# The router's logits computed in the attention's program instead of in a block of their own

## The chip, the core and the metric

One NeuronCore of one Trainium2 chip runs the whole kernel. The time is device microseconds of one execution; for each kernel the median of several runs counts. Five engines work side by side, each through its own list of instructions: TensorE (PE; its weight loads are shown as PEld), VectorE (DVE), ScalarE (ACT), GpSimd (POOL) and SyncE (SP), which here only issues DMAs. They wait for each other through semaphores.

## What is computed

A decoder layer on 64 sequences of 128 tokens, width 256, that is 8192 rows: causal self-attention with 16 heads, residual and layer norm; cross-attention, residual and layer norm; then a mixture of 8 experts (two per token, limited capacity), residual and layer norm.

```python
x = _layernorm(x + attn(x, w_in, w_out))
x = _layernorm(x + xattn(x, ctx, ctx, Wq, bq, Wk, bk, Wv, bv, Wo, bo))
# inside the expert part:
probs = softmax(x @ Wr + br, axis=-1)      # Wr is 256 x 8: the logits
gates, ids = top_k(probs, 2)
```

The change is about `x @ Wr + br`, which stands between the second layer norm and the choice of experts.

## The kernel before, in words

`decoder_layer` runs three stages one after the other: `attention_layers` (both attentions), `logits_block`, and `moe` (`route_block` and the experts). Each is a `Block`: a program for every engine, with a barrier at its end, so that no engine begins the next block before all have finished this one.

**Attention.** The rows are worked on in groups of 512 (G). There are 16 groups a layer, so 32 in all (`groups`), 64 half-groups (`halves_of`, indexed by u) and 128 sets of heads and rows (`sets`, indexed by k). The order of the instructions is written out by hand in each engine's program. Behind the loop over the sets stand the last steps. On TensorE (lines 470 to 475): `weigh(127)`, `set_back(126)`, `output(62)`, `set_back(127)`, `output_back(63)`, `output(63)`. A half-group ends so: TensorE turns the normalised heads back (`output_back`), ScalarE copies them as fp32r (`copy_out`), VectorE makes the rest (`rest_o`), TensorE multiplies with the output weights (`output`), VectorE adds the residual and takes the statistics (`residual`, `deviation`), GpSimd makes the inverse deviation, and ScalarE scales (`normalise`). SyncE stores the half-group to two tensors in HBM, `rows` and `total` (`store`, line 157).

SyncE's queue is in order. In the last group (g = 31) it calls `load_for_logits` (line 189): the identity, the router's matrix, the bias, and the first four groups of finished rows (`LOGIT_LOADS` = 4, 512 KB each). Then it issues the stores of half-groups 62 and 63 and waits for the landing of the last four stores, and the block ends.

**Logits.** `logits_block` (line 853) has 16 groups of 512 rows. A group takes these steps: TensorE turns the rows with 8 transposes into two PSUM banks (line 925, `lg_T`); ScalarE copies both as fp32r (line 950); VectorE subtracts for the rests (line 969); TensorE multiplies with the matrix, split into two parts, in 4 matmuls (`logits_of`, line 904); ScalarE adds the bias (line 943); TensorE turns the result back (`back`, line 914); VectorE adds the two parts (`take`, line 959). TensorE's order is turn(g), logits_of(g-1), back(g-2). The matrix is split on VectorE at the start of the block (lines 961 to 965), and TensorE waits for that before its first transpose. SyncE loads groups 4 to 15 into a ring of four, each when the group four before it has been turned (line 884), and then clears 128 spare rows of both tensors and loads `iota8` (lines 887 to 889).

PSUM has eight banks. The attention uses all of them (`A` has four, `B` and `C` two each), and so does the logits' block.

Of the kernel before, what the change touches and what calls it, by code (L numbers as in the profile page):

```python
# [38 lines left out]
def attention_layers(nc, layer_groups, x_in, x_turned, ctx_turned, x1, x2_outs, w_self, w_cross, consts, logits_inputs):  # L39
# [7 lines left out]
    with ExitStack() as c:  # L47
# [48 lines left out]
        C = [c.enter_context(nc.psum_tensor(f"{tag}C{i}", [P, G], FP32)) for i in range(2)]  # L96

# [41 lines left out]
        def _(sp):  # L139
# [59 lines left out]
            for g in range(groups):  # L199
# [19 lines left out]
        def _(pe):  # L219
# [598 lines left out]
E = 8  # L818
# [34 lines left out]
def logits_block(nc, tiles, rows_dram, sum_dram, inputs, logits, iota8, iota8_dram):  # L853


    groups = tiles // NB
    LOADS = LOGIT_LOADS
    with ExitStack() as c:
        wr_s = c.enter_context(nc.sbuf_tensor("lg_wr_s", [P, HALVES, 2, E], FP32R))
        zero = c.enter_context(nc.sbuf_tensor("lg_zero", [P, D + E], FP32))  # L860
        xT = c.enter_context(nc.sbuf_tensor("lg_xT", [P, 2, 2, HALVES, G], FP32R))
        lT = c.enter_context(nc.sbuf_tensor("lg_lT", [2 * E, 2, G], FP32))
        tb = [c.enter_context(nc.psum_tensor(f"lg_T{i}", [P, G], FP32)) for i in range(4)]
        lb = [c.enter_context(nc.psum_tensor(f"lg_L{i}", [2 * E, G], FP32)) for i in range(2)]
        bb = [c.enter_context(nc.psum_tensor(f"lg_B{i}", [P, NB, 2, E], FP32)) for i in range(2)]
        ident, wr, br, x2, const_in, x_loaded = (inputs[name] for name in ("ident", "wr", "br", "x2", "const_in", "x_loaded"))
        wr_hi = c.enter_context(nc.semaphore("lg_wr_hi"))
        wr_ready = c.enter_context(nc.semaphore("lg_wr_ready"))
        zero_made = c.enter_context(nc.semaphore("lg_zero_made"))
        zeroed = c.enter_context(nc.semaphore("lg_zeroed"))  # L870
        t_full = c.enter_context(nc.semaphore("lg_t_full"))
        a_copied = c.enter_context(nc.semaphore("lg_a_copied"))
        d_copied = c.enter_context(nc.semaphore("lg_d_copied"))
        l_full = c.enter_context(nc.semaphore("lg_l_full"))
        l_done = c.enter_context(nc.semaphore("lg_l_done"))
        b_full = c.enter_context(nc.semaphore("lg_b_full"))
        b_done = c.enter_context(nc.semaphore("lg_b_done"))
        block = c.enter_context(nc.Block())

        @block.sync  # L880
        def _(sp):
            for g in range(LOADS, groups):
                sp.wait_ge(t_full, g - LOADS + 1)
# [6 lines left out]
            sp.wait_ge(zeroed, 48)  # L890

        @block.tensor
        def _(pe):
            pe.wait_ge(const_in, 48)
            pe.wait_ge(wr_ready, 1)

# [1137 lines left out]
```

## Time and profile before

| | us |
|---|---|
| median of 3 runs | 1586.39 |
| lowest, highest | 1585.27, 1587.44 |
| profiled execution | 1587.09 |
| its span, first to last instruction | 1585.4 |
| mean granted TensorE clock, share of full | 0.946 |

Busy over the span: TensorE 90%, VectorE 64%, ScalarE 63%, GpSimd 39%.

| stretch of the trace, us | stage |
|---|---|
| 0 to 921 | attention, both layers |
| 921 to 924 | last stores land, barrier |
| 924 to 965 | logits |
| 965 to 1071 | routing |
| 1071 to 1585 | experts |

A row of the timeline gives the start and the length of an instruction, or of several of one kind in a row (x8), its engine, its line in the kernel, the tile written and the tiles read. In brackets stands how long the engine had been idle before it, and what ended that. PEclk is TensorE's granted clock as a share of 2.4 GHz.

### The profile page before, as it was taken

To read this page: it belongs to the slowest core of one execution; us is meant where nothing else is said; L and a number is where in the kernel's file an instruction comes from. 1 tells how busy PE (TensorE), PEld (TensorE's weight loads), DVE (VectorE), ACT (ScalarE), POOL (GpSimd) and SP (SyncE) were. 2 spreads that over 40 slices of the span, in tenths; PEclk is the share of its full clock that TensorE was granted. 3 is DMA by queue.
4 is the path that set the end of the run, shared out by engine and by line. 5 is a ranking of instruction groups with operands and counts; after the bars stand their busy time and mean duration, and the time that the engine had idled before them with its cause. 6 is when DMAs were issued, how large, how long until landed. Compare 5 with 4: busy or idle time off the path is not lost. (4 is left out here: it accounts for less than half of the span.)

```text
span 1585.4 us, 43757 instructions
## 1 busy us (share of the span) xinstructions
PE 1424.7 (90%) x17886; PEld 1198.1 (76%) x17886; DVE 1019.1 (64%) x2266; ACT 990.9 (63%) x1456; POOL 619.9 (39%) x688
## 2 busy tenths in 40 slices
PE   7999999999999999999999773158999999999990
PEld 5777777777777777777777652048999999999980
DVE  5666666666677777777777647884454454454582
ACT  4677777777777677777767554205565565565563
POOL 2644444454452322222232100013455455455485
PEclk9999999999999999999999976558999999999995
DMA  6021222122221222222221174003443443443464
GB/s 195 22 62 62 62 62 61 44 61 62 62 62 57 82 66 82 82 82 82 74 79 43 58 212 102 0 11 101 97 105 48 99 102 49 100 103 50 97 240 180
DMA packets 115142, 130.72 MB, mean 82 GB/s; under 512 B 26650, under 2 KB 97084, under 8 KB 114944
## 3 DMA queue, kind: packets, MB, share of 16 engines
q1 hardware_dynamic: 100288, 106.18, 21.5%
q0 software_dynamic: 14656, 21.74, 7.9%
q8 instruction: 144, 2.36, 0.6%
q14 instruction: 54, 0.44, 0.1%
HBM read 83.73 MB, written 44.16 MB: 81 GB/s over the span
## 5 line engine op out<-in xcount | busy, mean ns | idle before, releaser
L527 ACT ACTIVATE at_pr<-at_A 128x2048 f32<-128x2048 f32 x128 | 240.8, 1881 | 145.5 <-PE at_A L347 145.5
L622 DVE TENSOR_REDUCE at_mx<-at_A 128x12 f32<-128x1536 f32 x128 | 224.7, 1755 | 57.6 <-PE at_A L312 54.0
L767 POOL TENSOR_SCALAR_AFFINE_SELECT at_pr<-at_pr 128x2048 f32<-128x2048 f32 x64 | 128.6, 2010 | 204.9 <-ACT at_pr L527 204.8
L1839 POOL DMA_INDIRECT total<-ex_o,ids x70 | 115.8, 1654 | 187.5 <-DVE ex_o L1767 172.5
L1708 DVE TENSOR_TENSOR ex_hT<-ex_h,ex_hT 128x384 fp32r<-128x384 f32 (+1 forms) x192 | 113.0, 589 | 98.9 <-ACT ex_hT L1641 84.9
L658 DVE TENSOR_TENSOR at_oT<-at_C,at_oT 128x512 fp32r<-128x512 f32 x64 | 44.3, 692 | 164.9 <-ACT at_oT L540 164.9
L347 PE MATMUL at_A<-at_qp,at_kt 32*128 32x256 f32 x2048 | 139.8, 388 | 0.0
L362 PE MATMUL at_C<-at_pr,at_v 128*32 128x128 f32 x4096 | 138.3, 276 | 1.0 <-ACT at_oq L534 1.0
L1640 ACT ACTIVATE ex_h<-ex_U,ex_b 128x384 f32<-128x384 f32 (+1 forms) x192 | 116.3, 606 | 33.3 <-PE ex_U L35 27.4
L362 PEld LDWEIGHTS at_C<-at_pr,at_v 128*32 128x32 f32 x4096 | 104.0, 109 | 43.3 <-issue 42.1
L35 PE MATMUL ex_U<-ex_xT,ex_w_even 128*128 128x384 f32 (+1 forms) x576 | 115.3, 360 | 5.1 <-ACT ex_hT L1641 3.5
L774 POOL TENSOR_SCALAR at_shift<-at_mv 128x2 f32<-128x2 f32 x64 | 14.7, 230 | 264.9 <-DVE at_mv L686 262.3
L35 PE MATMUL ex_D<-ex_w_even,ex_hT 128*128 128x256 f32 (+1 forms) x960 | 117.2, 281 | 0.2
L35 PE MATMUL ex_D<-ex_w_odd,ex_hT 128*128 128x256 f32 (+1 forms) x960 | 116.6, 281 | 0.3
L35 PEld LDWEIGHTS ex_D<-ex_w_even,ex_hT 128*128 128x128 f32 (+1 forms) x960 | 115.1, 184 | 1.8 <-DVE ex_raw L1762 1.5
L1615 ACT CAST ex_xT<-ex_T 128x384 fp32r<-128x384 f32 (+1 forms) x46 | 21.0, 507 | 152.5 <-PE ex_T L1559 150.6
L35 PEld LDWEIGHTS ex_D<-ex_w_odd,ex_hT 128*128 128x128 f32 (+1 forms) x960 | 115.1, 184 | 1.4 <-DVE ex_raw L1762 0.9
L1641 ACT ACTIVATE ex_hT<-ex_U,ex_b 128x384 fp32r<-128x384 f32 (+1 forms) x192 | 114.7, 597 | 0.0
L35 PEld LDWEIGHTS ex_U<-ex_xT,ex_w_even 128*128 128x128 f32 x576 | 106.6, 195 | 10.0 <-ACT ex_hT L1641 3.9
L35 PE MATMUL ex_U<-ex_xT,ex_w_odd 128*128 128x384 f32 (+1 forms) x576 | 111.0, 351 | 0.0
L35 PE MATMUL at_B<-at_wo,at_oT 128*128 128x256 f32 x768 | 108.0, 290 | 1.4 <-DVE at_oT L658 1.4
L1823 POOL DMA_INDIRECT ex_xg<-rows,ids x77 | 97.5, 1266 | 28.6 <-issue 21.5
(245 smaller groups left out, 3067.9 us busy)
## 6 DMA issues: line engine op xcount, KB each, us to landing
ex_w_in<-in_w SPq DMA_DIRECT2D x16, 1024.0 KB
at_turned<-in_x_turned SPq DMA_DIRECT2D x16, 512.0 KB, 4.6
at_x<-in_x SPq DMA_DIRECT2D x16, 512.0 KB, 4.0
x<-at_y SPq DMA_DIRECT2D x32, 256.0 KB, 2.3
at_x<-x SPq DMA_DIRECT2D x16, 512.0 KB, 3.9
at_turned<-in_ctx_turned SPq DMA_DIRECT2D x16, 512.0 KB, 4.6
rows<-at_y SPq DMA_DIRECT2D x32, 256.0 KB, 2.2
total<-at_y SPq DMA_DIRECT2D x32, 256.0 KB, 3.1
```

Source lines behind the costliest of these rows:

```text
L35: last = nc.tensor.matmul(out, pick_l(left, a), pick_r(right, b), start=(start and n == 0), stop=(stop and n == 2))
L347: last = nc.tensor.matmul(A[:, i, n, :, :], kt[rows, g % 2, half, tok], qp[rows, g % 2, half, :, tok], start=False, stop=(n == 1), skip_gr ...
L362: last = nc.tensor.matmul(b[32 * j:32 * j + VW, (2 * n + quad) * P:(2 * n + quad + 1) * P], v[:, g % 2, 2 * np_ + n, half * HEADS_HALF + 4 ...
L527: nc.scalar.activation(pr[:, k % 2].rearrange("p i n a q -> p (i n a q)"), A[:].rearrange("p i n a q -> p (i n a q)"), ACT.Exp).then_inc(e ...
L622: nc.vector.tensor_reduce(mx[:, k % 2, 0:12], A[:, 0:3].rearrange("p i n a k -> p (i n a) k"), AX, ALU.max).then_inc(max_done, 1)
L658: nc.vector.tensor_tensor(oT[:, u % 2, 1].rearrange("p t n -> p (t n)"), C[1][:, :], oT[:, u % 2, 0].rearrange("p t n -> p (t n)").bitcast ...
L767: nc.gpsimd.affine_select(out=t, in_=t, compare_op=ALU.is_ge, fill=0.0, base=0, pattern=[[0, 16], [1, P]], channel_multiplier=-1).then_inc ...
L1640: nc.scalar.activation(h[:, m % HR, 0:n], U[m % UP][:, 0:n], ACT.Silu, bias=b1[:, j, m:m + 1])
L1641: nc.scalar.activation(hT[:, par(j, ch), 0, m, 0:n], U[m % UP][:, 0:n], ACT.Silu, bias=b1[:, j, m:m + 1]).then_inc(u_done, 1)
L1708: nc.vector.tensor_tensor(hT[:, par(j, ch), 1, m, 0:n], h[:, m % HR, 0:n], hT[:, par(j, ch), 0, m, 0:n].bitcast(FP32), ALU.subtract).then_ ...
L1823: nc.gpsimd.indirect_dma_start(xg[0:n, xg_of(s), b, :], None, rows_dram, bass.IndirectOffsetOnAxis(ap=ids[0:n, e, at:at + 1], axis=0), bou ...
L1839: nc.gpsimd.indirect_dma_start(sum_dram, bass.IndirectOffsetOnAxis(ap=ids[0:n, e, at:at + 1], axis=0), o[0:n, pr, b, :], None, bounds_chec ...
```

## The change

- The logits' programs become functions (`logits_programs`) that `attention_layers` calls from its own engine programs. The block `logits_block` and its barrier are gone. The PSUM banks of the logits are those of the attention: the turned rows lie in `A`, the logits in `B[1]` and `C[0]`, their transposes in `C[1]` and `B[0]`. The turned copies `xT` use the attention's `sT`.
- Groups 0 and 1 are turned, copied and split between the attention's last steps. The other 14 groups follow behind these steps, in the same order as before.
- `load_for_logits` is called in the group before the last (`groups - 2`).
- The clearing of the spare rows and the load of `iota8` move up, to between the last two stores; so do the loads of groups 4 and 5. The other loads follow the last store.
- The matrix is split behind `normalise_set(126)`. Before its third turn TensorE waits for the last residual.

```diff
@@ SyncE, in attention_layers
-                if g == groups - 1:
+                if g == groups - 2:
                     load_for_logits()
+            def load_later(i):
+                for u in (2 * (layer_groups + i), 2 * (layer_groups + i) + 1):
+                    sp.wait_ge(y_stored[u % 4], stored_before(u + 4))
+                load_rows(sp, i)
+
             store(halves_of - 2)
+            clear_rest(sp)
+            load_later(LOGIT_LOADS)
+            load_later(LOGIT_LOADS + 1)
             store(halves_of - 1)
+            for i in range(LOGIT_LOADS + 2, layer_groups):
+                load_later(i)
             for u in range(halves_of - 4, halves_of):
                 sp.wait_ge(y_stored[u % 4], stored_before(u + 4))
+            rest_cleared(sp)
@@ TensorE
             set_back(sets - 1)
+            turn_rows(pe, 0)
             output_back(halves_of - 1)
+            turn_rows(pe, 1)
             output(halves_of - 1)
+            tensor_program(pe, lambda engine: engine.wait_ge(res_done, halves_of))
@@ ScalarE
             copy_o(sets - 1)
+            copy_rows(act, 0)
             copy_out(halves_of - 1)
             normalise(halves_of - 2)
-            normalise(halves_of - 1)
+            copy_rows(act, 1)
+            scalar_program(act, lambda: normalise(halves_of - 1))
@@ VectorE
             normalise_set(sets - 2)
+            split_matrix(dve)
             residual(halves_of - 2)
             deviation(halves_of - 2)
             normalise_set(sets - 1)
+            rest_of_rows(dve, 0)
             rest_o(halves_of - 1)
+            rest_of_rows(dve, 1)
             residual(halves_of - 1)
             deviation(halves_of - 1)
+            vector_program(dve)
@@ new, in logits_programs
+    def load_rows(sp, g):
+        sp.wait_ge(turned, g - LOADS + 1)
+        sp.dma_start(x2[:, g % LOADS], rows_dram[g * G:(g + 1) * G, 0:D] ...
+    def clear_rest(sp):
+        sp.wait_ge(wr_ready, 1)
+        sp.dma_start(rows_dram[groups * G:groups * G + P, :], zero[:]).then_inc(zeroed, 16)
+        sp.dma_start(sum_dram[groups * G:groups * G + P, :], zero[:, 0:D]).then_inc(zeroed, 16)
+        sp.dma_start(iota8[:], iota8_dram).then_inc(zeroed, 16)
+    def tensor_program(pe, last_sum):
...
+        pe.wait_ge(wr_ready, 1)
+        logits_of(0)
+        last_sum(pe)
+        for g in range(2, groups):
+            turn_rows(pe, g)
+            logits_of(g - 1)
+            back(g - 2)
+        logits_of(groups - 1)
+        back(groups - 2)
+        back(groups - 1)
+    def scalar_program(act, last_normalise):
...
+        add_bias(0)
+        last_normalise()
+        for g in range(2, groups):
+            copy_rows(act, g)
+            add_bias(g - 1)
+        add_bias(groups - 1)
+    def vector_program(dve):
...
+        for g in range(2, groups):
+            rest_of_rows(dve, g)
+            take(g - 2)
+        take(groups - 2)
+        take(groups - 1)
@@ decoder_layer
-            logits_block(nc, tokens // P, rows, total, inputs, logits, iota8, ins["iota8"])
```

`turn_rows`, `copy_rows`, `rest_of_rows`, `logits_of`, `back`, `add_bias` and `take` hold the instructions of the old block for one group, with the waits they had.

## Rows read from the trace of the kernel before

**Rows 1.** Busy time of each engine by stretch, with granted clock (PEclk) and DMA

```profile
core 0: us, PE busy (x) PEld busy (x) DVE busy (x) ACT busy (x) POOL busy (x), PEclk, DMA share, GB/s
...
909.09:911.11 2.02, 0.00 (x1) 0.01 (x1) 1.86 (x7) 0.00 (x0) 0.45 (x2) 1.00 0.44 70
911.11:913.16 2.05, 0.65 (x4) 0.41 (x4) 0.69 (x1) 1.36 (x3) 0.91 (x2) 0.69 0.97 336
913.16:916.09 2.93, 2.93 (x12) 2.64 (x12) 0.00 (x0) 0.21 (x1) 0.00 (x0) 0.50 1.07 308
916.09:924.15 8.06, 0.01 (x1) 0.00 (x0) 1.70 (x6) 1.09 (x2) 1.36 (x4) 0.50 0.55 189
924.76:928.85 4.09, 3.65 (x17) 3.28 (x18) 1.29 (x2) 1.48 (x3) 0.00 (x0) 0.50 0.21 43
928.85:932.87 4.02, 4.02 (x29) 2.75 (x29) 2.68 (x5) 2.98 (x6) 0.00 (x0) 0.99 0.91 249
932.87:965.23 32.36, 30.89 (x215) 19.94 (x213) 18.95 (x42) 21.93 (x40) 0.00 (x0) 1.00 0.60 168
```

**Rows 2.** Timeline (start, us, engine line op) of TensorE over the attention's last steps

```profile
906.97 1.68 PE L35 MATMUL at_B<-at_wo,at_oT 128*128 128x256 f32 x12
...
911.11 0.66 PE L387 MATMUL at_C<-at_ident,at_on 128*128 128x128 f32 x4 [2.02 <-DVE at_on L653]
...
913.16 2.93 PE L35 MATMUL at_B<-at_wo,at_oT 128*128 128x256 f32 x12 [1.40 <-DVE at_oT L658]
```

**Rows 3.** Timeline of VectorE and ScalarE over the same steps

```profile
908.69 0.69 DVE L671 TENSOR_TENSOR at_y<-at_B,at_x 128x512 f32<-128x512 f32 x1 [0.72 <-PE at_B L35]
...
911.80 0.59 ACT L540 CAST at_oT<-at_C 128x512 fp32r<-128x512 f32 x1 [4.58 <-PE at_C L387]
...
912.28 1.09 ACT L545 ACTIVATE at_y<-at_y,at_shift,at_rstd 128x256 f32<-128x256 f32 x2
912.42 0.69 DVE L658 TENSOR_TENSOR at_oT<-at_C,at_oT 128x512 fp32r<-128x512 f32 x1 [1.36 <-ACT at_oT L540]
...
916.13 0.69 DVE L671 TENSOR_TENSOR at_y<-at_B,at_x 128x512 f32<-128x512 f32 x1 [3.02 <-PE at_B L35]
...
919.60 1.09 ACT L545 ACTIVATE at_y<-at_y,at_shift,at_rstd 128x256 f32<-128x256 f32 x2 [6.23 <-POOL at_shift L779]
```

**Rows 4.** Timeline of the logits block, from its first copy

```profile
926.79 1.07 ACT L950 CAST lg_xT<-lg_T 128x512 fp32r<-128x512 f32 x2 [6.10 <-PE lg_T L925]
927.41 1.29 DVE L969 TENSOR_TENSOR lg_xT<-lg_T,lg_xT 128x512 fp32r<-128x512 f32 x2 [2.75 <-ACT lg_xT L950]
...
930.86 1.07 ACT L950 CAST lg_xT<-lg_T 128x512 fp32r<-128x512 f32 x2 [0.19 <-PE lg_T L925]
...
932.87 1.17 PE L904 MATMUL lg_L<-lg_xT,lg_wr_s 128*16 128x512 f32 x4
...
934.32 1.09 PE L925 MATMUL lg_T<-lg_ident,lg_x 128*128 128x128 f32 x8
...
960.39 1.17 PE L904 MATMUL lg_L<-lg_xT,lg_wr_s 128*16 128x512 f32 x4
```

**Rows 5.** Timeline of the SyncE queue around the moved issues

```profile
896.23 0.36 SPq L161 DMA_DIRECT2D rows<-at_y  x1
...
913.40 0.36 SPq L161 DMA_DIRECT2D rows<-at_y  x1
...
920.72 0.36 SPq L161 DMA_DIRECT2D rows<-at_y  x1
...
951.89 0.50 SPq L887 DMA_DIRECT2D rows<-lg_zero  x1
...
952.44 1.32 SPq L888 DMA_DIRECT2D total<-lg_zero  x1
```

**Rows 6.** DMAs of line L196, the first four loads of rows, issue to landing

```profile
DMA to landing us min/median/max: 3.6/5.5/7.4
```

**Rows 7.** DMAs of line L884, the twelve later loads of rows, issue to landing

```profile
DMA to landing us min/median/max: 3.5/3.9/4.9
```

More of the change, by code:

```diff
@@ new lines, in rest_cleared, with turn_rows @@
+    def rest_cleared(sp):
+        sp.wait_ge(zeroed, 48)
+    def turn_rows(pe, g):
+        if g == 0:
+            pe.wait_ge(const_in, 48)
+        pe.wait_ge(x_loaded[g % LOADS], 16 * (g // LOADS + 1))
+        if g >= 2:
+            pe.wait_ge(d_copied, 2 * (g - 1))
+        for half in range(HALVES):
+            for n in range(NB):
+                last = nc.tensor.matmul(T[2 * (g % 2) + half][:, n * P:(n + 1) * P],
+                                        x2[:, g % LOADS, n, half * P:(half + 1) * P], ident[:],
+                                        start=True, stop=True, is_transpose=True)
+        last.then_inc(turned, 1)
@@ new lines, in tensor_program, with logits_of, back @@
+    def tensor_program(pe, last_sum):
+        def logits_of(g):
+            pe.wait_ge(a_copied, 2 * g + 2)
+            pe.wait_ge(d_copied, 2 * g + 2)
+            if g >= 2:
+                pe.wait_ge(l_done, g - 1)
+            for part in range(2):
+                for t in range(HALVES):
+                    last = nc.tensor.matmul(lb[g % 2], wr_s[:, t, :, :].rearrange("p a e -> p (a e)"),
+                                            xT[:, g % 2, part, t, :],
+                                            start=(part == 0 and t == 0), stop=(part == 1 and t == HALVES - 1))
+            last.then_inc(l_full, 1)
+        def back(g):
+            pe.wait_ge(l_done, g + 1)
+            if g >= 2:
+                pe.wait_ge(b_done, g - 1)
+            for n in range(NB):
+                last = nc.tensor.matmul(bb[g % 2][:, n, :, :].rearrange("p a e -> p (a e)"), lT[:, g % 2, n * P:(n + 1) * P],
+                                        ident[0:2 * E, 0:2 * E],
+                                        start=True, stop=True, is_transpose=True)
+            last.then_inc(b_full, 1)
+        pe.wait_ge(wr_ready, 1)
[8 more added lines that the diff above has]
+        back(groups - 1)
@@ new lines, in copy_rows, with add_bias @@
+    def copy_rows(act, g):
+        if g == 0:
+            act.wait_ge(const_in, 48)
+        act.wait_ge(turned, g + 1)
+        if g >= 2:
+            act.wait_ge(l_full, g - 1)
+        for half in range(HALVES):
+            nc.scalar.copy(xT[:, g % 2, 0, half, :], T[2 * (g % 2) + half]).then_inc(a_copied, 1)
+    def scalar_program(act, last_normalise):
+        def add_bias(g):
+            act.wait_ge(l_full, g + 1)
+            if g >= 2:
+                act.wait_ge(b_full, g - 1)
+            nc.scalar.activation(lT[:, g % 2, :], lb[g % 2], ACT.Identity, bias=br[:, 0:1]).then_inc(l_done, 1)
+        add_bias(0)
[4 more added lines that the diff above has]
+        add_bias(groups - 1)
@@ new lines, in split_matrix, with rest_of_rows @@
+    def split_matrix(dve):
+        nc.vector.memset(zero[:], 0.0)
+        dve.wait_ge(const_in, 48)
+        nc.vector.tensor_copy(wr_s[:, :, 0, :], wr[:]).then_inc(wr_hi, 1)
+        dve.wait_ge(wr_hi, 1)
+        nc.vector.tensor_tensor(wr_s[:, :, 1, :], wr[:], wr_s[:, :, 0, :].bitcast(FP32), ALU.subtract).then_inc(wr_ready, 1)
+    def rest_of_rows(dve, g):
+        for half in range(HALVES):
+            dve.wait_ge(a_copied, 2 * g + half + 1)
+            nc.vector.tensor_tensor(xT[:, g % 2, 1, half, :], T[2 * (g % 2) + half],
+                                    xT[:, g % 2, 0, half, :].bitcast(FP32), ALU.subtract).then_inc(d_copied, 1)
@@ new lines, in vector_program, with take @@
+    def vector_program(dve):
+        def take(g):
+            dve.wait_ge(b_full, g + 1)
+            nc.vector.tensor_reduce(logits[:, g * NB:(g + 1) * NB, :], bb[g % 2].rearrange("p n a e -> p n e a"),
+                                    AX, ALU.add).then_inc(b_done, 1)
+        for g in range(2, groups):
[3 more added lines that the diff above has]
+        take(groups - 1)
+    return load_rows, clear_rest, rest_cleared, turn_rows, tensor_program, copy_rows, scalar_program, split_matrix, rest_of_rows, vector_program
```

136 lines of the change are left out of this document (24 added, 112 removed).

## The prediction

> **What bounds the kernel now.** I began with the busy time by stretch, because an average over the whole kernel hides the seam between attention and router [rows 1]. Up to 909 us TensorE is busy and its clock is at 1.00 (2.4 GHz). Then come 15 us in which it does little: 0.00 busy in 2.02, 0.65 in 2.05, one product of 2.93 us at a clock of 0.50 (1.2 GHz), and 0.01 busy in the 8.06 us to 924.15. Only after that does the logits' work start, again at 0.50, and from 932.87 it runs 32.36 us with TensorE busy for 30.89.
>
> The timelines then say what each part waits for. In the attention's tail a single half-group goes round: transpose back at 911.11, copy at 911.80, rest at 912.42, output product at 913.16, residual at 916.13, last normalise at 919.60 [rows 2, 3]. That is a chain of dependences, with every engine mostly idle. In the logits' loop the product of one group begins 2.29 us after that of the one before it ((960.39 - 932.87) / 12), and TensorE has no gap there, so TensorE sets the pace [rows 4]. The seam between them is pure delay: the last normalise ends at 920.69, and the copies of the third group of rows, the first point from which the loop runs evenly, start at 930.86 [rows 3, 4]. Those 10.2 us hold two stores and their landing, the barrier, the matrix split, and groups 0 and 1 turned at the half clock.
>
> **The change part by part.** All starts of the new kernel are estimates, worked out from the rows named, on the clock of the trace of before.
>
> *Loads one group sooner.* Three constants and four loads of 512 KB are issued after the store of half-group 59, near 884 us. The next store comes at 896.23 [rows 5] and the slowest of these loads took 7.4 us [rows 6], so they have landed before anything asks for them. Cost nothing; cover some 8 us. They also leave the queue free later.
>
> *Matrix split* (VectorE: a clear, a copy, a subtraction of small tiles). It goes in front of the residual at 908.69, before which VectorE sat 0.72 us idle [rows 3]. The first loop step of the old block cannot begin until this is done (TensorE started at 924.76, the block at 924.15 [rows 1]), so it took at most 0.6. It fits: cost nothing, 0.6 if the cover were gone.
>
> *Group 0 turned, copied, split.* Eight transposes at full clock take 1.09 [rows 4] and go from about 909.1 into the 2.02 us in which TensorE is idle [rows 1]: done by 910.2, before output_back at 911.11. ScalarE copies for 1.07, 910.2 to 911.3, before copy_out at 911.80: 0.5 us to spare. VectorE subtracts for 1.29 from about 911.1 (it has just released output_back) to 912.4, and rest_o starts at 912.42 [rows 3]. This is the thinnest cover, nearly zero; I book 0.0, with 0.3 as the upper bound if a copy is late.
>
> *Group 1.* Transposes follow output_back, 911.8 to 912.9; output starts at 913.16, so hidden. ScalarE's copies stand behind normalise(62), which runs 912.28 to 913.37, so they run 913.3 to 914.4. Rests follow 0.62 after the copies (927.41 against 926.79 [rows 4]) and take 1.29: 913.9 to 915.15. Here VectorE is late for once: the residual that it must do next is queued behind them.
>
> *The last output product.* At full clock it takes 1.68, as at 906.97; it took 2.93 at half clock [rows 2]. The clock fell after TensorE had been idle 2.02 us and busy 0.65 of the following 2.05 [rows 1]. The 16 transposes fill both gaps to about 0.9 us idle and 0.3 us idle, so I take the full clock. The product then ends at 914.84 rather than 916.09, the residual could start at 914.9, and starts at 915.1 behind the rests: 1.0 sooner than 916.13. All that follows up to the last normalise keeps its 3.47 us, so that starts at 918.6.
>
> *The seam.* ScalarE goes straight from normalise(63) to the copies of group 2. Two instructions in a row overlap by 0.1 (912.28 against 911.80 + 0.59 [rows 3]), so these start at 918.6 + 1.09 - 0.1 = 919.6 instead of 930.86: **11.3 us sooner**. Of this 10.3 is the seam and 1.0 the clock. Behind the output product TensorE has logits(0) 1.17, then the wait for the last residual (about 915.8), turn(2) 1.09, logits(1) 1.17, back(0) 0.4 and turn(3) 1.09 [rows 4]. It is through near 919.6, and logits(2) comes 2.01 after the copies as before (932.87 - 930.86), at 921.6. Thus ScalarE's last normalise sets the start of the loop; TensorE waits 2 us for it.
>
> *The loop.* From there its operations, order and depth are the same, the rest is 32.36 us in both, and the route and expert stages start from the same state. They shift as a block.
>
> *SyncE's queue.* The store of half-group 62 (913.40) is now followed by the three clearing DMAs and the loads of groups 4 and 5; the last store stands behind these. The clears took 0.50 and 1.32 for two of them [rows 5]; with some 0.5 for each other issue the queue is free near 917.8, and the last store's data are ready at 919.7. Cost nothing; cover 1.9 us. No engine waits for that store but the loads issued behind it.
>
> *Rows in time.* Load 4 is issued near 916.8 and needed at 934.32 - 11.3 = 923.0 [rows 4]. The landings are 3.5 to 4.9 in the loop [rows 7] and up to 7.4 with four in a row [rows 6]: 920.7 to 924.2. Load 6 must follow the last store, so it is issued near 920.7, and is needed two periods later than load 4, at 927.6; it lands between 924.2 and 928.1. I take the median of the rows where loads queue, 5.5, since the last store's 512 KB lie before it: no wait. Upper end 1.2 us.
>
> The Trainium skill ("DMA: Bandwidth & Descriptors", Queues, rings and completion order) says that each DMA engine consumes its descriptors in ring order, which speaks against this arrangement: load 6 cannot pass the last store. This trace does not show the order by itself. By the skill's fixed cost of about 2.0 us and 27 GiB/s for each of 16 engines an estimate for 1 MB is 4.3 us, which would put load 6 at 925.0, in time; the sum would not change.
>
> **Sum.** 1587.09 (the profiled execution: span 1585.4 and 1.7 around it) - 11.3 = 1575.8. The median of the three runs, 1586.39, is 0.7 below the profiled execution, so for the median: **1575.1 us**.
>
> **Rivals.**
>
> *The clock falls in the new gap.* My own sum leaves TensorE idle for 2 us between turn(3) and logits(2), as long as the gap of 2.02 after which it fell before. Against it: here 6 us of dense work stand before and TensorE stays busy after. Where it falls, TensorE sets the pace and pays: the 16 first transposes took 3.65 at half clock [rows 1] against 2 x 1.09. It rose again after 4 us of work (from 924.76 to near 928.9, 0.99 in the next stretch). Loss: 4.1 x (1 - 2.18 / 3.65) = 1.7. Time 1576.8.
>
> *The clock falls where it did.* If the transposes do not hold it, the output product stays 2.93 and the residual starts at 916.13: the gain is the seam alone, 10.3. The rests of group 1 are then covered. TensorE has 16 transposes and two products behind it at half clock, but 3 us of waiting to absorb them. Time 1576.1. For it: what I add is small work. Against: it was at 1.00 up to 909 with gaps.
>
> *A late load.* Load 4 or 6 holds the loop for up to 1.2: 1576.3.
>
> *Slower than before.* TensorE runs the whole loop at 0.50, for instance after a fall at the new gap from which it does not rise. A period would be 2.29 x 3.65 / 2.18 = 3.8, 1.5 more for each of 14 groups, 21 in all, less 11.3: 1596. It decides from the point where 8 groups run at half clock (8 x 1.5 = 12). Against it: in the trace it rose after 4 us of such work, and stayed up.
>
> *The change does nothing for time.* This would need the last store's landing or the barrier to lie on the path still. ScalarE has no wait between normalise(63) and the copies but for the turned rows, so only a hidden stall at the end, where SyncE waits for clears issued 35 us earlier, could do so. I see none. Time 1586.4.
>
> **How the numbers follow.** Forecast 0.50; fall in the gap 0.24; fall as before 0.12; late load 0.06; slower 0.02; nothing gained 0.02; and 0.04 for a later stage that moves by a few us for reasons not in these rows. A measurement of this kernel tells about 0.2% (3.2 us) from no change. Faster by more takes all the first four and half of the last: 0.94; same 0.03; slower 0.03. The range takes in both clock cases, the late load on top of either, and the 1.1 us by which single runs of before lie around their median: 1573.4 to 1578.2.
>
> **What would show it.** In the new profile: PEclk 1.00 over the output product and its length 1.68; the last residual near 915.1 and the last normalise near 918.6; copies of group 2 within 1.0 us of that start; logits(2) near 921.6; a period of 2.29; the block's end near 953.9; the expert stage as long as before. The prediction is wrong if VectorE's rests push rest_o beyond 912.7, if a turn waits for its rows, or if the period is longer.

## The result, and the profile after

| | before | after |
|---|---|---|
| median of 6 runs each, us | 1586.32 | 1578.65 |
| lowest, highest | 1585.27, 1587.77 | 1574.62, 1581.2 |
| ratio, with its 95% interval | | 0.9949 (0.9934 to 0.9965) |
| profiled execution | 1587.09 | 1579.99 |
| its span | 1585.4 | 1578.2 |
| mean granted clock of TensorE | 0.946 | 0.948 |

The change gives 7.7 us, where 11.2 were forecast, and 1578.65 lies 0.45 above the top of the range. The six runs also lie further apart (6.6 us) than those of before (2.5 us), and their times go with their clocks: the fastest, 1574.62, ran at a mean of 0.951, the slowest, 1581.2, at 0.947.

The last steps of the attention in the changed kernel, as a timeline (start, length, engine and line, tiles, count; in brackets the idle time and what ended it). It answers to [rows 2, 3].

```profile
908.98 1.04 PE L918 MATMUL at_A<-lg_ident,lg_x 128*128 128x128 f32 x8
...
911.03 1.28 DVE L989 TENSOR_TENSOR at_sT<-at_A,at_sT 128x512 fp32r<-128x512 f32 x2
...
911.66 1.04 PE L918 MATMUL at_A<-lg_ident,lg_x 128*128 128x128 f32 x8
...
912.48 0.69 DVE L677 TENSOR_TENSOR at_oT<-at_C,at_oT 128x512 fp32r<-128x512 f32 x1 [0.17 <-ACT at_oT L557]
...
913.23 1.70 PE L35 MATMUL at_B<-at_wo,at_oT 128*128 128x256 f32 x12 [0.53 <-DVE at_oT L677]
...
915.14 0.68 DVE L690 TENSOR_TENSOR at_y<-at_B,at_x 128x512 f32<-128x512 f32 x1
...
918.60 1.09 ACT L562 ACTIVATE at_y<-at_y,at_shift,at_rstd 128x256 f32<-128x256 f32 x2 [2.03 <-POOL at_shift L802]
919.60 1.05 ACT L964 CAST at_sT<-at_A 128x512 fp32r<-128x512 f32 x2
...
921.58 1.87 PE L931 MATMUL at_B<-at_sT,lg_wr_s 128*16 128x512 f32 x4 [2.31 <-ACT at_sT L964]
```

Both turns sit in the gaps, the output product takes 1.70 instead of 2.93, the last normalise starts at 918.60, the copies of group 2 at 919.60 and the product of group 2 at 921.58. The forecast said 918.6, 919.6 and 921.6. Yet that product takes 1.87, not 1.09 or 1.17.

The same stretches as [rows 1], of the changed kernel:

```profile
core 0: us, PE busy (x) PEld busy (x) DVE busy (x) ACT busy (x) POOL busy (x), PEclk, DMA share, GB/s
909.20:911.15 1.95, 0.82 (x8) 0.58 (x6) 1.85 (x8) 1.04 (x2) 0.45 (x2) 1.00 0.05 13
911.15:913.20 2.05, 1.53 (x12) 1.29 (x12) 1.85 (x3) 1.38 (x4) 0.91 (x2) 1.00 0.01 3
913.22:915.00 1.78, 1.77 (x14) 1.62 (x15) 1.06 (x2) 1.18 (x3) 0.00 (x0) 1.00 0.38 133
919.25:921.55 2.30, 0.02 (x1) 0.00 (x0) 1.36 (x3) 2.30 (x5) 0.00 (x0) 0.94 1.02 358
921.55:928.05 6.50, 6.47 (x24) 3.56 (x24) 2.87 (x6) 2.79 (x6) 0.00 (x0) 0.50 0.73 211
928.05:956.80 28.75, 27.29 (x189) 17.78 (x188) 16.30 (x36) 18.94 (x35) 0.00 (x0) 1.00 0.50 142
```

The clock holds through the attention's tail. It falls in the gap of 2.3 us between turn(3) and logits(2): TensorE then starts only 24 matmuls in the next 6.50 us, at 0.50. This is the first rival of the prediction, with a longer stretch at half clock than it allowed.

To compare executions part by part I measure from fixed marks in each timeline: **A**, from ScalarE's first normalise of the last group of rows (half-group 60) to that of half-group 61; **B**, from the same start to the router's first instruction on ScalarE (the part the change is about, A included); **E**, the experts' start, from the first product into `ex_U` to the first into `ex_D`.

| trace | start of A | A | B | E | span |
|---|---|---|---|---|---|
| before | 895.11 | 10.52 | 70.41 | 26.16 | 1585.4 |
| after | 893.67 | 12.02 | 63.42 | 27.06 | 1578.2 |

From B's end to the experts' first product it is 105.61 and 105.66, and from the first product into `ex_D` to the end 488.11 and 488.39. So the 7.2 us of span are: B 6.99 less, everything ahead of the last group 1.44 less, E 0.90 more, and 0.33 more in the rest.

B should have lost 11.3. A holds 1.5 of what is missing: A is work that the change doesn't touch, and in it the clock fell. First before, then after:

```profile
895.11:905.63 10.52, 8.27 (x163) 6.46 (x166) 5.88 (x15) 6.16 (x8) 1.36 (x4) 1.00 0.15 52
```

```profile
893.67:905.69 12.02, 9.76 (x163) 7.85 (x166) 5.89 (x15) 6.16 (x8) 1.36 (x4) 0.86 0.13 46
```

and its product at the start, on the timeline:

```profile
894.18 2.91 PE L35 MATMUL at_B<-at_wo,at_oT 128*128 128x256 f32 x12
```

The work is the same on every engine and only TensorE's part is longer, with an output product of 2.91. The 1.44 us ahead of the last group are a fall too, one that the trace of before has near its start and the other has not (0.76 against 1.00). It comes and goes with the execution: of the 19 traces of this study the 10 that have it reach the last group at 894.12 to 895.12, and those without it at 893.36 to 893.86, or at 894.23 in one with another fall just ahead. First before, then after:

```profile
8.00:15.00 7.00, 4.38 (x12) 3.45 (x13) 6.51 (x14) 1.27 (x2) 1.42 (x1) 0.76 1.05 377
```

```profile
8.00:15.00 7.00, 4.58 (x19) 3.23 (x18) 6.57 (x14) 1.86 (x3) 1.48 (x1) 1.00 1.06 383
```

E has two slow groups of 24 products in both kernels. The first opens it (6.54 before, 6.86 after), while the clock is still at the 0.50 of the routing. The second stands at its end, behind a wait of 3.53 and 3.00; it takes 6.04 before and 6.97 in the changed kernel, where a group at full clock takes 4.46. First before, then after:

```profile
1071.13 6.54 PE L35 MATMUL ex_U<-ex_xT,ex_w_even 128*128 128x384 f32 x24 [1.58 <-PEq L992]
...
1091.41 6.04 PE L35 MATMUL ex_U<-ex_xT,ex_w_even 128*128 128x384 f32 x24 [3.53 <-ACT ex_hT L1641]
```

```profile
1062.75 6.86 PE L35 MATMUL ex_U<-ex_xT,ex_w_even 128*128 128x384 f32 x24 [1.58 <-PEq L1021]
...
1083.00 6.97 PE L35 MATMUL ex_U<-ex_xT,ex_w_even 128*128 128x384 f32 x24 [3.00 <-ACT ex_hT L1670]
```

### The profile page after: what moved, and what is told of

Its sections match the earlier page's. It is cut to its first block and busy times, and to the rows that moved or that the text cites. A ratio compares the mean times of both kernels' runs of the same rounds, so it can differ in the third digit from the quotient of the medians.

```text
span 1578.2 us, 43757 instructions
## 1 busy us (share of the span) xinstructions
PE 1427.3 (90%) x17886; PEld 1198.4 (76%) x17886; DVE 1019.1 (65%) x2266; ACT 991.2 (63%) x1456; POOL 619.4 (39%) x688
```

## The experiments

**My theory:** the seam is worth the 11.3 us of the forecast, and what is missing is TensorE's clock: a fall in the new gap, and in this execution one in the last group. **Rivals:** the loop or the loads cost more than booked; the interleaved steps hold up the attention's tail; the experts' start is worse with this kernel. A, B and E are taken from one profiled execution of each kernel; medians and ratios from its timed runs. All kernels below compute the whole result. Where products of zeros are added, they write into a PSUM bank that nobody reads just then.

### The same kernel again, and with the new gap filled

The first kernel is the changed one, unaltered. The second fills the gap with ten products of zeros (`FILL` = 10), 512 columns each, behind turn(3):

```diff
             turn_rows(pe, g)
+            if g == 3:
+                for _ in range(FILL):
+                    nc.tensor.matmul(L[0][:, :], warm[:, 0:P], warm[:, :], start=True, stop=True)
             logits_of(g - 1)
```

> The changed kernel again, beside the others, for more of its times with their clocks. The gap theory (TensorE idles 2.3 us before the product of group 2, and in some executions its clock falls to 0.50 there for one or two stretches of 3.4 us) expects a median of 1576 to 1580, a spread of 5 us or more, and times that go with the mean granted clock: in the six runs so far 0.951 gave 1574.6 and 0.947 gave 1580.6 to 1581.2. A rival that puts the spread on the transfers expects times that do not go with the clock.

> Ten products of zeros (512 columns each, 2.1 us at full clock) stand in the 2.3 us gap behind the fourth turn; nothing else changes. Gap theory: PEclk is 1.00 from 909 to the end of the logits, the last product of the logits comes 37 us after the last normalise begins or sooner (it was 955.27 + 0.42 - 918.60 in the changed kernel with the fall, 2.6 less without), and the median is 1 to 2.5 us below the changed kernel's. Rival, that the fall has its cause before the gap or is only a matter of when the chip looks: it falls as before, and the products of zeros at half clock cost up to 2 us more. Rival, that the loop lost its time to late rows: no change from the changed kernel.

Measured: the changed kernel 1570.46 against 1581.87 of the kernel before beside it, ratio 0.9940 (0.9926 to 0.9953), 11.4 us. Filled: 1570.22, 0.9928 (0.9914 to 0.9941), 11.65 us. The medians do not tell them apart, though 1 to 2.5 us were expected; the spread does, 4.8 us against 1.4. The median of the unaltered kernel was expected at 1576 to 1580. But the kernel before takes 4.5 us less here too than in the first comparison, so I take this for another chip (which one the first comparison ran on is not on record; all later ones are).

The trace of this execution of the changed kernel is the case without a fall. The product behind the gap takes 1.09, and in the 6.54 us from there TensorE starts 45 matmuls where it started 24 in 6.50:

```profile
919.77 1.09 PE L931 MATMUL at_B<-at_sT,lg_wr_s 128*16 128x512 f32 x4 [2.31 <-ACT at_sT L964]
```

```profile
917.45:919.76 2.31, 0.01 (x1) 0.02 (x1) 1.38 (x3) 2.31 (x5) 0.00 (x0) 1.00 1.03 358
919.76:926.30 6.54, 6.53 (x45) 4.23 (x46) 4.07 (x9) 4.53 (x9) 0.00 (x0) 1.00 0.96 277
```

With the gap filled:

```profile
917.12 1.09 PE L918 MATMUL at_A<-lg_ident,lg_x 128*128 128x128 f32 x8
918.05 2.32 PE L955 MATMUL at_B<-at_warm 128*128 128x512 bf16 x10
920.53 1.08 PE L933 MATMUL at_B<-at_sT,lg_wr_s 128*16 128x512 f32 x4 [0.16 <-issue]
```

| trace | A | B | E |
|---|---|---|---|
| changed kernel, no fall | 10.52 | 59.10 | 20.78 |
| gap filled | 10.52 | 59.10 | 20.88 |

70.41 - 59.10 = **11.31 us**: with the clock up, the change brings what the sum said. The fill costs nothing: the product after it waits 0.16, and starts 26.41 behind the start of A in both traces.

### More executions of the changed kernel

One trace with a fall and one without say little on how often it comes, so the pair was run again on three more chips (9, 2 and 11; the runs above are from chip 1), the last time with the waits of the last group filled too (the edit is shown further down).

> The changed kernel once more, beside the kernel with its gap filled and the one with the copies first, for a comparison within one call (the first call found 11.4 us and the blind runs 7.7 us of gain). Gap theory: 7 to 11.5 us below the kernel before, with a spread of 4 us or more; executions with the higher mean clock are the faster ones. From the last group's first normalise to the first instruction of the routing the trace shows 59.1 us if the clock stays up, 60.6 if it falls in the last group, about 62 if it falls in the gap, 63.4 if in both (before: 70.4).

> The changed kernel with ten products of zeros in the gap. Gap theory: its slowest executions are faster than the slowest of the changed kernel by 2 us or more, its fastest equal to the fastest of the changed kernel within 0.5 us, its median 0 to 3 us lower. Rival, that the difference of 3.6 us between the first two comparisons came from the chips alone: same median and same spread as the changed kernel.

> The changed kernel a third time. 7.5 to 11.5 us below the kernel before. If the smaller gain of the blind runs belonged to chips on which the experts' start stalls (26 us from the first to the last of their first-layer products instead of 21), a chip of that kind gives 7 to 9 and one of the other kind 9.5 to 11.5; if it was the chance of where the clock falls, either kind gives either.

> The gap filled. Gap theory: 1 to 3 us below the changed kernel on a chip with that stall, and no execution slower than the changed kernel's slowest less 2 us. From the last group's first normalise to the routing 59.1 us, or 60.6 if the clock falls in the last group.

> The changed kernel a fourth time. On a chip with the stall at the experts' start (kernel before near 1586): 7 to 10 us of gain and times spread over 4 us or more, if the two places in which the clock falls are the reason for the blind runs' 7.7. On one without it: 9.5 to 11.5, as three times before.

> The changed kernel with both places filled (ten products of zeros in the gap, 19 in the last group's waits), beside the changed kernel on the same chip. 11 to 11.7 us below the kernel before on either kind of chip, spread 2 us or less. If the kind of chip, not the clock, made the blind runs' shortfall: no better than the changed kernel beside it.

| run | before beside it | this | ratio (95%) | A | B | fall at the gap |
|---|---|---|---|---|---|---|
| changed, 2nd | 1581.10 | 1571.58 | 0.9934 (0.9921 to 0.9948) | 12.03 | 63.36 | yes |
| changed, 3rd | 1581.61 | 1570.56 | 0.9925 (0.9912 to 0.9939) | 12.02 | 62.02 | yes |
| changed, 4th | 1581.24 | 1571.48 | 0.9939 (0.9925 to 0.9952) | 10.51 | 60.56 | yes |
| gap filled, 2nd | 1581.10 | 1570.33 | 0.9932 (0.9918 to 0.9945) | 10.52 | 59.29 | no |
| gap filled, 3rd | 1581.61 | 1570.12 | 0.9922 (0.9909 to 0.9936) | 10.52 | 59.21 | no |
| both filled | 1581.24 | 1570.40 | 0.9928 (0.9914 to 0.9942) | 10.52 | 59.12 | no |

The differences of B are made of few sizes. In the 4th, A is undisturbed and B is 1.46 above 59.10: a fall in the gap costs **1.5** when the low stretch is short. In the 3rd, A is 1.50 over and B 2.92: a fall in each place, 1.4 for the gap. In the 2nd and in the first profile after, A is 1.5 over and B 4.3: the low stretch behind the gap is the longer one and costs **2.8**. The short one, in the 4th, begins only some 1.9 us behind the gap, leaves the first product untouched and hits what follows:

```profile
920.81 1.09 PE L931 MATMUL at_B<-at_sT,lg_wr_s 128*16 128x512 f32 x4 [2.30 <-ACT at_sT L964]
...
922.17 1.50 PE L918 MATMUL at_A<-lg_ident,lg_x 128*128 128x128 f32 x8
923.33 2.05 PE L931 MATMUL at_C<-at_sT,lg_wr_s 128*16 128x512 f32 x4
...
925.85 1.21 PE L918 MATMUL at_A<-lg_ident,lg_x 128*128 128x128 f32 x8
```

Over the four comparisons, 20 runs of the changed kernel lie at a median of 10.4 below the kernel before beside them (from 6.6 to 13.0). The 15 runs with the gap alone filled lie at 11.4 (9.5 to 13.05), 0.2, 1.3 and 0.4 better in the three pairs, each within its intervals. A gain of the fill in the median is thus not clear of noise. The spread is smaller in each pair: 1.4 against 4.8, 1.9 against 2.9, 2.4 against 3.8, and with both filled 3.0 against 4.2, where 2 or less was expected. That fits a gap in which the clock falls often, not always, and for 1.5 as well as for 2.8. The third filled trace has a fall of its own ahead of A, at 887.6.

### Only the last group filled

The gap stays open; 19 products of zeros stand in the waits of TensorE in the last group. The one added wait lets the bank that they write be read first.

```diff
+                if k == sets - 2:
+                    fill(3)
                 if k % 2 == 0:
                     turn_max(k)
+                if k == sets - 3:
+                    pe.wait_ge(v_done, 2 * groups)
+                    fill(3)
                 if k + 1 < sets:
                     maxima(k + 1)
+                if k == sets - 1:
+                    fill(5)
                 if k >= 2:
                     set_back(k - 2)
+                if k == sets - 3:
+                    fill(5)
                 scores(k)
...
+            fill(3)
             weigh(sets - 1)
```

> The changed kernel with the 19 products of zeros in the last group's waits and none in the gap: the two places taken apart. The fall in the last group cannot come (1.5 us where it did), the one in the gap can (2.8 us): a median 0 to 1.5 us below the changed kernel, a spread still of 3 us or more. If the gap does not matter: as the kernel with both.

Measured: 1570.11 against 1581.61, 0.9927 (0.9914 to 0.9941). A is 10.52, undisturbed, and B 60.63: 1.53 over 59.10, a short fall in the gap.

```profile
919.95 1.08 PE L945 MATMUL at_B<-at_sT,lg_wr_s 128*16 128x512 f32 x4 [2.31 <-ACT at_sT L978]
...
921.30 1.84 PE L932 MATMUL at_A<-lg_ident,lg_x 128*128 128x128 f32 x8
```

So the two falls are separate: the one at the gap came here without one in the last group, as in the 4th above. With this gap open there are seven traces in all, the one with late loads below among them, and the clock fell at it in six. In the five with the gap filled, and in the four without such a gap (below), it fell at none. For the last group the traces say less: without products of zeros there the clock fell within A in 5 of 14, with them in none of 5, which chance could do as well.

### Both filled, on a chip like the first

> The changed kernel with the ten products of zeros in its gap, and 19 more in five waits of TensorE in the attention's last group (near 887, 889, 893, 900 and 905 us), where its clock fell at 893.9 in one trace of the changed kernel and at 893.4 in one with late loads. Gap theory: no stretch at 0.50 between 30 us and the end of the logits; the median as that of the kernel with the ten products alone, or up to 1 us lower, spread 2 us or less. If products of zeros in these waits hold up the real work behind them: up to 1 us slower.

Measured, on chip 3: 1575.82 against 1587.07, 0.9933 (0.9920 to 0.9947), 11.25 us; the spread is 1.6. A 10.52, B 59.09, E 26.72, which answers to 26.16 of before. Here the kernel before takes its 1587 again, and E is 26 to 27 as in the first comparison, not 21. With the clock held, the gain on such a chip is the 11.2 that was forecast.

### The turns not interleaved

```diff
             set_back(sets - 1)
-            turn_rows(pe, 0)
             output_back(halves_of - 1)
-            turn_rows(pe, 1)
             output(halves_of - 1)
+            turn_rows(pe, 0)
+            turn_rows(pe, 1)
```

ScalarE's copies of groups 0 and 1 go behind the last normalise, VectorE's rests behind the last deviation.

> One program as in the changed kernel, loads as early, but groups 0 and 1 are turned after the last output product, and copied and split after the last normalise and the last statistics: the merge without the interleaving. My working: copies of group 0 at 920.6, the product of group 2 near 927 instead of 921.6 (before: 932.87), so a gain of 5 to 6 us over the kernel before, a median about half way between it and the changed kernel. If the barrier alone were the gain: as fast as the changed kernel. If the interleaving alone were it: no gain over the kernel before.

Measured: 1583.03 against 1587.07, 0.9977 (0.9968 to 0.9986), 4.0 us, where 5 to 6 were expected. The output product is back at 2.93, and the loop's first product comes at 927.93, behind three more steps in a row:

```profile
912.86 2.93 PE L35 MATMUL at_B<-at_wo,at_oT 128*128 128x256 f32 x12 [1.40 <-DVE at_oT L678]
...
919.28 1.09 ACT L562 ACTIVATE at_y<-at_y,at_shift,at_rstd 128x256 f32<-128x256 f32 x2 [6.21 <-POOL at_shift L803]
920.28 2.02 ACT L965 CAST at_sT<-at_A 128x512 fp32r<-128x512 f32 x4
...
925.51 1.08 ACT L965 CAST at_sT<-at_A 128x512 fp32r<-128x512 f32 x2 [1.03 <-PE at_A L919]
...
927.93 1.17 PE L932 MATMUL at_B<-at_sT,lg_wr_s 128*16 128x512 f32 x4
```

B is 65.90: 4.5 less than before, 6.8 more than with the turns interleaved. Dropping the block and its barrier alone is the smaller part of the gain; the turns in the gaps are the larger, since they take two groups out of the way and hold the clock.

### The kernel before with its seam filled

This separates the clock from the order of the work. To the kernel before, products of zeros are added and nothing else:

```diff
             set_back(sets - 1)
+            fill(8)
             output_back(halves_of - 1)
+            fill(5)
             output(halves_of - 1)
+            fill(35)
```

> The kernel before, with products of zeros in the gaps of its seam: 8 before the last output_back, 5 before the last output, 35 behind it (0.21 us each at full clock). Gap theory: PEclk is 1.00 through the seam, the last output product takes 1.7 instead of 2.93 (1.2 us sooner), the first turns of the logits run at full clock (about 2 us less), in all 2 to 3.3 us faster than the kernel before. What is left of the changed kernel's gain, 8 us, is then the seam's waits. If the clock is no cause of the seam's length: no change.

Measured: 1585.51 against 1587.07, 0.9989 (0.9980 to 0.9998), 1.6 us, under what was expected. The output product does take 1.70, and the 16 first transposes run at full clock, but TensorE then waits for ScalarE's copies:

```profile
914.24 1.70 PE L35 MATMUL at_B<-at_wo,at_oT 128*128 128x256 f32 x12 [0.32 <-DVE at_oT L665]
...
924.89 1.94 PE L932 MATMUL lg_T<-lg_ident,lg_x 128*128 128x128 f32 x16 [1.39 <-DVE lg_wr_s L972]
...
928.10 1.09 PE L911 MATMUL lg_L<-lg_xT,lg_wr_s 128*16 128x512 f32 x4 [1.27 <-ACT lg_xT L957]
```

The last normalise starts 1.25 sooner, once the 1.5 of a fall in the last group (A 12.01) is taken off. From there to routing it is 45.34 instead of 45.92: 0.6 for turns that became 1.7 shorter. So the clock was worth 1.25 in the tail, as in the prediction (914.84 against 916.09, of which 0.2 goes to the rests ahead of the residual and 1.0 was booked), and little in the seam.

### Rows loaded in the last group, as before

```diff
-                if g == groups - 2:
+                if g == groups - 1:
                     load_for_logits()
```

> The first four loads of rows and the three constants go back to the last group (issued near 909.6); all else as in the changed kernel. My working of cost and cover: the first load lands 3.6 us or more after its issue, so the first turn starts at 913.2 or later instead of 908.9, and the output product behind it 4 us late; the median is 3 to 6 us above the changed kernel's. If the sooner loads were not needed: no change.

Measured: 1577.02 against 1581.87, 0.9968 (0.9956 to 0.9980), 4.85 us: 6.6 of the gain lost, a little over what was expected. TensorE waits for the rows of group 0 right in the attention's tail, and its clock is down at the end of that wait (0.50 from 914.1 to 917.4), so both the transfer and the clock are in these 6.6 us:

```profile
910.34 2.30 SPq L199 DMA_DIRECT2D lg_x<-rows  x4
...
914.11 1.94 PE L918 MATMUL at_A<-lg_ident,lg_x 128*128 128x128 f32 x8 [5.29 <-DMA lg_x<-rows]
```

The turn holds up `output_back`, and so the whole chain of the last half-group. Booked as "cost nothing", the earlier load is in truth a condition of the rest.

### The copies ahead of the last normalise

The prediction said that ScalarE's last normalise sets the start of the loop. If so, the copies of group 2 should go first:

```diff
@@ TensorE
-        last_sum(pe)
         for g in range(2, groups):
             turn_rows(pe, g)
             logits_of(g - 1)
+            if g == 3:
+                last_sum(pe)
             back(g - 2)
@@ ScalarE
-        last_normalise()
         for g in range(2, groups):
             copy_rows(act, g)
             add_bias(g - 1)
+            if g == 2:
+                last_normalise()
```

> ScalarE copies group 2 and adds the bias of group 1 ahead of the last normalise, and TensorE waits for the last residual only before it writes the bank that the residual reads (before the second transpose back). Gap theory: the product of group 2 starts near 918.9 instead of 921.6, TensorE has no gap, the clock stays at 1.00, and the median is 2.7 + 1 to 2.5 = 4 to 5 us below the changed kernel's, 1572 to 1575. If the last normalise were not what sets the start of the loop: no change. If the copies now hold up the last normalise and its store and the rows behind it: less than 2 us.

> The copies of group 2 ahead of the last normalise. 12 to 14 us below the kernel before, and 1.5 to 2.5 us below the kernel with the filled gap: the loop starts as soon as TensorE is ready, and ScalarE is then half a microsecond late once.

> The copies of group 2 ahead of the last normalise (the fastest kernel so far), with the same 19 products of zeros in the last group's waits. Expected: 13.5 to 15 us below the kernel before, with a spread of 2 us or less. If the fall in the last group is rare or hidden, the same as without them.

Measured: 1568.09, ratio 0.9916 (0.9902 to 0.9929), 13.8 us; again 1568.21, 0.9915 (0.9901 to 0.9928), 12.9 us; with the last group filled, on a chip like the first, 1573.77, 0.9915 (0.9901 to 0.9928), 13.3 us, just under the 13.5 to 15 expected of it. In the trace of the first:

```profile
915.17 1.07 ACT L965 CAST at_sT<-at_A 128x512 fp32r<-128x512 f32 x2 [0.20 <-PE at_A L918]
...
917.00 1.09 ACT L562 ACTIVATE at_y<-at_y,at_shift,at_rstd 128x256 f32<-128x256 f32 x2 [0.20 <-POOL at_shift L802]
917.18 1.18 PE L931 MATMUL at_B<-at_sT,lg_wr_s 128*16 128x512 f32 x4
...
923.90 1.09 PE L918 MATMUL at_A<-lg_ident,lg_x 128*128 128x128 f32 x8 [0.18 <-DMA lg_x<-rows]
...
926.84 1.09 PE L918 MATMUL at_A<-lg_ident,lg_x 128*128 128x128 f32 x8 [0.58 <-DMA lg_x<-rows]
```

The copies run in ScalarE's idle time, the normalise is no later for it, and the gap of 2.3 us on TensorE is gone. B is 57.66, and 56.78 in the second trace: 1.4 and 2.3 below 59.10. The 0.9 between them is mostly the 0.76 that TensorE waits for rows in the first. The loop has come so far forward that the loads are now just in time. In the gap's place no fill is needed, and the spread is 1.2 to 2.5. This is the fastest order of the study, ahead of both kernels.

### The experts' start kept warm

The first products of the experts run at half clock in every trace, so here 100 small products stand in the wait ahead of the experts, beside the copies first and the last group filled:

```diff
+            for _ in range(100):
+                nc.tensor.matmul(bn[0][:, 0:P], ones_h[:], same_h[:], start=True, stop=True)
             pe.wait_ge(x_loaded[0], 16 * parts[0])
```

> The copies first, the 19 products of zeros in the last group, and 100 small ones (128 columns) in the 9.9 us in which TensorE waits at the end of the routing for the first gathered rows, so that its clock may be up when the experts begin. In all traces so far the first 24 products of the experts took 6.1 to 6.9 us against 4.45 for the next 24. Clock theory: they take 4.5, and the median is 1.5 to 2.5 us below the same kernel without the 100, 15 to 16.5 us below the kernel before. If the clock falls again in the 1.6 us between the blocks: no change. If the small products are still running when the rows land: up to 1 us slower.

Measured: 1567.68 against 1581.10, 0.9910 (0.9896 to 0.9923), 13.4 us, where 15 to 16.5 were expected; the same without these products and without those in the last group is the 1568.21 above, on the same chip, 0.5 apart and within the intervals. The first transposes are at full clock, and TensorE waits 2.18 before them and 1.71 after; then the clock falls all the same:

```profile
1044.30 7.84 PE L1196 MATMUL rt_N<-rt_same_h,rt_ones_h 128*128 128x128 f16 x100
...
1054.33 0.88 PE L1200 MATMUL ex_T<-ex_ident,ex_xg 128*128 128x128 f32 x6 [2.18 <-DMA ex_xg<-rows,ids]
...
1056.92 6.91 PE L35 MATMUL ex_U<-ex_xT,ex_w_even 128*128 128x384 f32 x24 [1.71 <-PEq L1037]
```

The opening group of 24 takes 6.91, no less than the 6.54 and 6.86 of the first two traces, and E is 20.94. In this trace the full clock carried over the wait of 2.18, but no longer over the 1.71 behind it.

## Why the prediction was right and wrong, by its own steps

**Right, to a tenth or two: the seam and the tail.** 10.3 for the seam and 1.0 for the output product make 11.3; the six traces of the changed kernel, filled or not, with no fall in A or at the gap give B 59.09 to 59.29, 11.1 to 11.3 under before. That the starts in the first trace match the forecast to a hundredth is luck: this trace is 1.44 early at the start of A and loses 1.50 in it. Counted from the start of A, where no clock fell (the second trace of the changed kernel), the last normalise starts at 23.42, the copies at 24.42 and the product at 26.41; the forecast gives 23.5, 24.5 and 26.5. ScalarE's last normalise did set the loop's start: moving it behind the copies gave 2 us more.

**Right: the covers.** The split of the matrix fits into VectorE's idle time (908.03 to 908.55, the residual at 908.75 behind TensorE). The thinnest one held: the rests of group 0 end at 912.31, and rest_o starts at 912.48 on ScalarE's copy. The last residual stands behind the rests of group 1, at 915.14 (915.1 was said). No turn waits for its rows in the traces of the changed kernel, so nothing here tests whether load 6 could have passed the last store. The Trainium skill ("TensorE: Matmul & The Clock Gate", Part 4) says that the full clock doesn't engage for transposes, since they don't count as TensorE being busy in the same way. By that the turns in the gaps would not have held the clock for the output product; here the granted clock is 1.00 with them in the gaps, in all 15 traces that have them there with their rows loaded in time, and falls at the same place where they are moved out of it (2.93 at 912.86). The measurement decides: these fp32 transposes do hold it.

**Right: the queue and the slower rivals.** SyncE issues the last store at 919.72, when the data are there. The loop rises to 1.00 and stays, so nothing runs at half clock to its end.

**Wrong: the chance of the fall in the new gap.** The prediction saw it, put 0.24 on it and took the clock up as its likeliest case, because 6 us of dense work stand before the gap. It fell in 6 of 7 traces with this gap. The reason given against it does not hold: a gap of 2.3 us on TensorE is enough after dense work, though it is no certainty either.

**Mis-sized: the price of that fall.** 1.7 was worked out from one low stretch of 4.1 us. Measured are 1.4 to 1.5, where the stretch is short, and 2.8 in the profile after, where the clock is 0.50 from 921.55 to 928.05.

**Wrong: "they shift as a block".** This step took all work outside the seam as the same in both. The work is; its clock isn't. The fall in the last group, ahead of every moved instruction, cost 1.5 in the profile after and in three other traces of kernels whose last group is unaltered in its computation (the changed kernel twice, late loads), but also in one of the kernel before with only its seam filled. So the change is not shown to cause it: it is a place where the clock may fall in either kernel. The experts' start was 0.9 longer, the second slow group above all (6.97 against 6.04). That too is no mark of the change: in the four other traces of the slower kind of chip E is 26.5 to 27.3, and the 27.3 belongs to the kernel before with only its seam filled. The range had nothing for either.

**Wrong: the top of the range, by its own terms.** It was to hold the fall in the gap (1576.8), a late load on top (1.2) and the 1.1 by which single runs lie apart. These add up to 1579.1, not to 1578.2, so what was left out of the range is in part a slip of adding. 1579.1 would have held the median, but not for the reason measured: no load was late; the fall in the last group and the longer low stretches took that room.

**Adding up the first comparison.** Forecast for B -11.3; fall in the last group +1.5; fall in the gap +2.8; makes -7.0, as in the table. The experts' start +0.9, the rest +0.3 and the start of the kernel -1.4 give the span's -7.2. The medians differ by 7.7. So in the profiled execution the 4.3 that B lacks are clock. For the median's miss of 3.5 this is an inference: only one of the six runs has a trace, and their times going with their mean clocks speaks for it.

**What stays open.** Where the 5 us between chips come from: E is 26 to 27 us on the chips where the kernel before takes 1586 to 1587, and 21 where it takes 1581 to 1582. TensorE waits there for 3.5 and 3.0 us ahead of the last of its four groups of products (3.53 at 1091.41, 3.00 at 1083.00). In the six traces of that kind ScalarE waits just before for something that the profile calls remote (2.9 us together in the trace of before), and in none of the 13 others; what that is was not isolated. Only one chip of that kind, chip 3, is on record. Nor did the unaltered changed kernel run a second time on a chip of that kind, so the step from 7.7 to 11.25 there rests on two comparisons, perhaps on two chips, and on the sums of their traces. Nor was it settled why the clock falls in the last group in some executions and holds in others with the same waits.

## What to carry to other kernels

When a seam is closed, look at the gaps left on TensorE, and count one of about 2 us as a possible fall of the clock, likely in this case, with a price from the trace's rows at either level: the same program then has several times, and a forecast needs them in its range. Fill such a gap with work that is due anyway, as the turned groups do here, or change the order so that it goes away (the copies ahead of the normalise, 2 us more); products of zeros into a free bank narrowed the spread here and are left where no such work exists. A load counted as free because it is early should be priced at its old place as well: here that was 6.6 of 11.4 us.

## What the runs showed of the hardware

- The same instructions gave different clocks: at the same gap of 2.3 us the granted clock stayed at 1.00 once and fell to 0.50 six times, twice a little behind the gap (0.8 and 1.9 us); the unaltered kernel alone has four of these falls in five traces. A fall cost 1.4 to 1.5 or 2.8 us.
- A fall can come where nothing was changed: 1.5 us in the last group of the attention, in 5 of the 14 traces in which its work is the same to the instruction.
- Chips differ here in one part of the kernel only: E 21 us on four, 26 to 27 on chip 3 and in the first comparison, while B's end to the experts' first product was 105.5 to 105.7 on all of them (105.0 with the products added there).
- Transposes count for the clock here: it stays at 1.00 with 16 of them in two gaps of 2 us (15 traces), and falls without them (the kernel before, and the turns not interleaved).
